# Score matmuls of both kinds in the two row halves, plain fp32 down products, and the gate copied by ScalarE and weighted by GpSimd

## The reference

```python
xn = layernorm(x)                                   # over the 128 channels
qkv = xn @ Wqkv + bqkv                              # 16 heads of depth 8
q, k = rope(q), rope(k)
scores = einsum('bhtd,bhsd->bhts', q, k) / sqrt(8)
attn = einsum('bhts,bhsd->bhtd', softmax(scores), v)  @ Wout + bout
r = sigmoid(xn @ gate_w + gate_b); top 2 of 16, values divided by their sum
hg, hu = xn @ experts_wg, xn @ experts_wu           # 16 experts of width 64
expert = sum over the two of r * ((silu(hg) * hu) @ experts_wd)
out = x + attn + xn + shared_mlp(xn) + expert       # shared_mlp: one more of width 64
```

## Time and profile before

| | |
|---|---|
| median of 3 runs | 239.06 us |
| the profiled execution | 239.08 us, of it 237.2 us span |
| TensorE busy | 212.7 us, 90% |
| VectorE busy | 186.9 us, 79% |
| GpSimd busy | 162.5 us, 69% |
| ScalarE busy | 135.3 us, 57% |
| chain that ended last | 64% TensorE, 18% VectorE |

### The profile page before, as it was taken

The page is one execution under the profiler, slowest core; times in us unless marked ns, Lnnn a source line. Parts: engine busy times, 40 slices in busy tenths (PEclk is TensorE's granted clock), DMA queues, the critical chain, the costliest instruction groups (busy, mean ns, idle before and its releaser), DMA issues.

```text
span 237.2 us, 4808 instructions
## 1 busy us (share of the span) xinstructions
PE 212.7 (90%) x1603; PEld 138.2 (58%) x1603; DVE 186.9 (79%) x407; ACT 135.3 (57%) x253; POOL 162.5 (69%) x245
## 2 busy tenths in 40 slices
PE   0485698889999999999999999999999999999993
PEld 0254454365565666665755656766766666676651
DVE  5897959999886888999858778998688878876521
ACT  2476111244458656665574766667676767666662
POOL 9185764799825479968938586979885874648722
PEclk9998789999999999999999999999999999999999
DMA  7924444630537340503662423206425550311101
GB/s 224 368 69 141 115 141 131 194 121 0 164 95 220 92 136 5 155 0 94 199 195 58 149 59 104 53 26 192 135 61 166 170 153 9 91 41 52 48 3 44
DMA packets 35953, 26.53 MB, mean 112 GB/s; under 512 B 4236, under 2 KB 30156, under 8 KB 35916
## 3 DMA queue, kind: packets, MB, share of 16 engines
q1 hardware_dynamic: 35292, 25.33, 35.9%
q10 hardware_dynamic: 636, 0.88, 1.0%
HBM read 18.53 MB, written 7.47 MB: 110 GB/s over the span
## 4 chain that ended last, share of the span: by engine, by line
PE 64%; DVE 18%; DMA 5%; SPq 4%; issue 3%; ACT 3%; POOL 1%; DVEq 0%; ACTq 0%; POOLq 0%
PE PV L553 11%; PE S2b L534 6%; PE S2a L534 5%; PE S1a L513 4%; DVE mx L1019 4%; PE S1b L513 4%; PE FB L391 3%; PE FA L393 3%; PE FA L391 3%; PE FA L392 3%; PE FB L393 3%; PE Y L391 3%; PE FB L392 3%; PE Y L392 2%; PE Y L393 2%
## 5 line engine op out<-in xcount | busy, mean ns | idle before, releaser
L749 ACT ACTIVATE probs<-S2b 128x512 f32<-128x512 f32 x62 | 37.0, 596 | 31.0 <-PE S2b L534 30.8
L1154 POOL TENSOR_TENSOR hid_lo<-gu,hid_hi 128x512 fp32r<-128x512 f32 (+1 forms) x27 | 34.7, 1286 | 23.5 <-ACT hid_hi L792 21.7
L1019 DVE TENSOR_REDUCE mx<-S1b 128x2 f32<-128x512 f32 x63 | 43.1, 684 | 7.8 <-PE S1b L513 7.7
L1019 DVE TENSOR_REDUCE mx<-S1a 128x2 f32<-128x512 f32 x65 | 44.5, 684 | 5.7 <-PE S1a L513 5.7
L1138 POOL TENSOR_TENSOR gu<-gu,wbc 128x512 f32<-128x512 f32 x32 | 41.0, 1282 | 11.5 <-DVE gu L1007 9.2
L749 ACT ACTIVATE probs<-S2a 128x512 f32<-128x512 f32 x62 | 37.1, 599 | 14.3 <-PE S2a L534 11.7
L553 PE MATMUL PV<-probs,vx 128*32 128x256 f32 x512 | 35.0, 384 | 0.9 <-ACT probs L749 0.9
L761 ACT ACTIVATE th<-FA 128x512 f32<-128x512 f32 (+1 forms) x36 | 21.5, 596 | 25.1 <-PE FA L393 24.8
L1028 DVE SCALAR_TENSOR_TENSOR th<-th,FA 128x512 f32<-128x512 f32 (+1 forms) x36 | 24.6, 683 | 10.9 <-ACT th L761 10.1
L513 PE MATMUL S1a<-k_hat,q_hat 96*128 96x256 bf16 x130 | 25.3, 275 | 0.7 <-DVE mx L1019 0.7
L513 PE MATMUL S1b<-k_hat,q_hat 96*128 96x256 bf16 x126 | 24.3, 273 | 1.4 <-DVE mx L1019 1.3
(11 more groups left out here) (171 smaller groups left out, 437.8 us busy)
## 6 DMA issues: line engine op xcount, KB each, us to landing
wbc<-route_w SPq DMA_DIRECT2D x64, 128.0 KB, 3.0
q_hat<-q_parts SPq DMA_DIRECT2D x32, 96.0 KB, 2.6
k_hat<-k_parts SPq DMA_DIRECT2D x32, 96.0 KB, 2.6
k_parts<-parts SPq DMA_DIRECT2D x8, 192.0 KB, 2.1
q_parts<-parts SPq DMA_DIRECT2D x8, 192.0 KB, 2.2
x_sb<-in_x SPq DMA_DIRECT2D x4, 256.0 KB, 4.1
q_parts<-parts SPq DMA_DIRECT2D x8, 128.0 KB, 2.1
k_parts<-parts SPq DMA_DIRECT2D x8, 128.0 KB, 2.1
```

What stands on the lines that cost most here:

```text
L749: nc.scalar.activation(probs[:, head % (2 * NQ), :], exp_bank(head)[:], ACT.Exp, scale=SCALE).then_inc(exp_done, 1)
L1019: nc.vector.tensor_reduce(mx[:, (q // QB) % 2, (q // 2) % 2, :, q % 2, i], S1[use % 2][:].rearrange("p (t s) -> p t s", t=SB), axis=AX.X, ...
L1154: nc.gpsimd.tensor_tensor(hid_lo[0:rows, m % 2, :], gu[0:rows, m % GU_SLOTS, :], hid_hi[0:rows, m % 2, :].bitcast(f32), ALU.subtract).then ...
```

## The change

- `k_hat` loses its copy for each parity and the zeros. A head's 48 score rows plus 3 rows of maxima or ones (`KALL` = 51) stand in rows 0 to 50 or in rows 64 to 114; which half is `score_row_half(q, i)`, so it alternates from step to step. The ones and the maxima take two DMAs each where they took one.
- TensorE issues a step's scores interleaved: first half of exp, first half of max, second half of exp, second half of max. The head of the maxima is the step's neighbour (`i ^ 1`), so that the two kinds read opposite row halves. Both banks are waited for ahead of the first of the four. Blocks 30 and 31 interleave two exponential heads.
- `down` is a plain fp32 matmul for all 36 chunks; `wd_hi`, `wd_lo`, `hid_hi`, `hid_lo` and what makes them are gone.
- From chunk 6 on, ScalarE copies FA to `gate` after the tanh (times 0.5 for c = 0) and with that frees FA; VectorE does one operation, (tanh + 1) * hu; GpSimd multiplies `gate` by the routing weight and then the product by `gate`.

```diff
-MROW = 2 * KROWS
+HROWS = 64
+KALL = KROWS + PARTS
...
+GATES_COPIED = CHLEAD
...
+def score_row_half(q, i):
+
+    return (q + i) % 2
...
-                sp.dma_start(k_hat[MROW:KALL, s], kones).then_inc(ld_kones, 16)
+                for r in range(2):
+                    sp.dma_start(k_hat[HROWS * r + KROWS:HROWS * r + KALL, s], kones).then_inc(ld_kones, 16)
...
-                sp.dma_start(q_hat[MROW:KALL, (h // 2) % 2, NQ * half:NQ * (half + 1), :],
-                             mT[0:MROWS * NQ, h % 2, :]).then_inc(max_ld[h % 4], 16)
+                for r in range(2):
+                    sp.dma_start(q_hat[HROWS * r + KROWS:HROWS * r + KALL, (h // 2) % 2, NQ * half:NQ * (half + 1), :],
+                                 mT[PARTS * NQ * r:PARTS * NQ * (r + 1), h % 2, :]).then_inc(max_ld[h % 4], 16)
...
+            def max_scores(bank, q, i, t):
+
+                j = i ^ 1
+                pair, slot, rows = NQ * ((q // 2) % 2) + j, (q // QB) % 2, HROWS * score_row_half(q, j)
+                return nc.tensor.matmul(bank[:, t * T:(t + 1) * T],
+                                        q_hat[rows:rows + KROWS, slot, pair, t * P:(t + 1) * P],
+                                        k_hat[rows:rows + KROWS, slot, pair, :], start=True, stop=True)
...
+            def exp_scores(bank, q, i, s):
+                pair, slot, rows = NQ * ((q // 2) % 2) + i, (q // QB) % 2, HROWS * score_row_half(q, i)
+                return nc.tensor.matmul(bank[:, s * T:(s + 1) * T],
+                                        k_hat[rows:rows + KALL, slot, pair, s * P:(s + 1) * P],
+                                        q_hat[rows:rows + KALL, slot, pair, :], start=True, stop=True)
+
+            def score_step(e, q, i):
+
+                exps, maxima = 0 <= e < FOUR_BANKS, 0 <= q < NBLK
+                if exps:
+                    s2 = free_exp_bank(e, i)
+                if maxima:
+                    s1 = max_bank(q, i)
+                for half in range(SB):
+                    if exps:
+                        scored = exp_scores(s2, e, i, half)
+                        if half == SB - 1:
+                            scored.then_inc(s2_ready, 1)
+                    if maxima:
+                        scored = max_scores(s1, q, i, half)
+                        if half == SB - 1:
+                            scored.then_inc(s1_ready, 1)
...
-                if n < PLAIN:
-                    pe.wait_ge(gu_weighted, n + 1)
-                    nc.tensor.matmul(Y[:], wd_sb[0:rows, c, :], gu[0:rows, n % GU_SLOTS, :],
-                                     start=c == 0, stop=c == NCH - 1).then_inc(down_done, 1)
-                    return
...
-                pe.wait_ge(hid_ready, n + 1 - PLAIN)
-                split_product(Y[:], wd_hi[0:rows, c, :], wd_lo[0:rows, c, :], hid_hi[0:rows, n % 2, :],
-                              hid_lo[0:rows, n % 2, :], c == 0, c == NCH - 1).then_inc(down_done, 1)
+                pe.wait_ge(gu_weighted, n + 1)
+                nc.tensor.matmul(Y[:], wd_sb[0:rows, c, :], gu[0:rows, n % GU_SLOTS, :],
+                                 start=c == 0, stop=c == NCH - 1).then_inc(down_done, 1)
...
-            act.wait_ge(ld_down, 32)
-            nc.scalar.activation(wd_hi[0:I, 0, :], wd_sb[0:I, 0, :], ACT.Copy)
-            nc.scalar.activation(wd_hi[:, 1:, :], wd_sb[:, 1:, :], ACT.Copy).then_inc(down_hi_ready, 1)
...
+                        if n >= GATES_COPIED:
+                            if n - 2 >= GATES_COPIED:
+                                act.wait_ge(gu_weighted, n - 1)
+                            nc.scalar.activation(gate[0:rows, n % 2, :], FA[0:rows, :], ACT.Copy,
+                                                 scale=0.5 if n % NCH == 0 else 1.0).then_inc(fa_read, 1)
...
-                        act.wait_ge(gu_weighted, n)
-                        if n - 3 >= PLAIN:
-                            act.wait_ge(down_done, n - 2)
-                        nc.scalar.activation(hid_hi[0:rows, (n - 1) % 2, :], gu[0:rows, (n - 1) % GU_SLOTS, :],
-                                             ACT.Copy).then_inc(hid_hi_ready, 1)
...
-            nc.vector.memset(k_hat[0:MROW, 0].rearrange("p a r t -> p (a r t)").bitcast(u32), 0).then_inc(hat_zeroed, 1)
...
+                            nc.vector.scalar_tensor_tensor(gu[0:rows, m % GU_SLOTS, :], th[0:rows, m % 2, :], 1.0,
+                                                           FB[0:rows, :], ALU.add, ALU.mult).then_inc(fb_read, 1)
...
-                    if i == 0 and n < NCHUNKS:
+                    if i == 0 and n < GATES_COPIED:
...
-            nc.gpsimd.memset(k_hat[0:MROW, 1].rearrange("p a r t -> p (a r t)").bitcast(u32), 0).then_inc(hat_zeroed, 1)
...
+            def weight_gate_and_product(m):
+
+                g, c = chunk_group(m)
                 rows = I if c == 0 else P
...
+                gates, product = gate[0:rows, m % 2, :], gu[0:rows, m % GU_SLOTS, :]
+                pool.wait_ge(fa_read, A_USE["hg", m] + 1)
+                if c:
+                    pool.wait_ge(wbc_ld[c - 1], 32 * (g + 1))
+                    after(nc.gpsimd.tensor_tensor(gates, gates, wbc[:, g % 2, c - 1, :], ALU.mult))
+                pool.wait_ge(fb_read, B_USE["hu", m] + 1)
+                nc.gpsimd.tensor_tensor(product, product, gates, ALU.mult).then_inc(gu_weighted, 1)
...
-                if PLAIN <= m < NCHUNKS:
-                    rows = I if m % NCH == 0 else P
-                    pool.wait_ge(hid_hi_ready, m + 1 - PLAIN)
-                    nc.gpsimd.tensor_tensor(hid_lo[0:rows, m % 2, :], gu[0:rows, m % GU_SLOTS, :],
-                                            hid_hi[0:rows, m % 2, :].bitcast(f32), ALU.subtract).then_inc(hid_ready, 1)
```

More of the change, by code:

```diff
@@ L186, in layer_kernel @@
         q_hat = sb("q_hat", [P, 2, H // 2, T], bf16)
-        k_hat = sb("k_hat", [P, 2, H // 2, 2, T], bf16)
+        k_hat = sb("k_hat", [P, 2, H // 2, T], bf16)
         mx = sb("mx", [P, 2, 2, SB, 2, NQ])
@@ L198, in layer_kernel @@
         th = sb("th", [P, 2, GT])
+        gate = sb("gate", [P, 2, GT])
         gu = sb("gu", [P, GU_SLOTS, GT])
-        hid_hi, hid_lo = sb("hid_hi", [P, 2, GT], f32r), sb("hid_lo", [P, 2, GT], f32r)
         yT = sb("yT", [P, 2, GT])
@@ L322, in load_hats @@
                 sp.wait_ge(scratch_done[slot], 16 * WRITES * (b // GB + 1))
-                if h < 4:
-                    sp.wait_ge(hat_zeroed, 2)
-                else:
+                if h >= 4:
                     sp.wait_ge(s2_ready, 2 * NQ * (h - 3))
                 for r in range(2):
-                    rows = slice(KROWS * r, KROWS * (r + 1))
+                    rows = slice(HROWS * r, HROWS * r + KROWS)
                     pairs = slice(NQ * half, NQ * (half + 1))
-                    for hat, dram in ((q_hat[rows, slot, pairs, :], q_dram), (k_hat[rows, slot, pairs, r, :], k_dram)):
+                    for hat, dram in ((q_hat[rows, slot, pairs, :], q_dram), (k_hat[rows, slot, pairs, :], k_dram)):
                         sp.dma_start(hat, dram[b, 2 * half + r].rearrange("j k t -> k j t")).then_inc(hat_ld[h % 4], 16)
@@ L504, in maxima_to_rows, with max_bank, free_exp_bank @@
                 last.then_inc(s1_ready, 1)
-            def max_scores(q, i):
-                b, r, hg = q // QB, q % 2, (q // 2) % 2
-                pair, slot = NQ * hg + i, b % 2
+            def max_bank(q, i):
                 if q % 2 == 0 and i == 0:
                     pe.wait_ge(hat_ld[(q // 2) % 4], 64 * (q // 8 + 1))
[L511 to L519, removed]
+                return take_s(("max", q * NQ + i))
+            def max_scores(bank, q, i, t):
[4 more added lines that the diff above has]
+                                        k_hat[rows:rows + KROWS, slot, pair, :], start=True, stop=True)
+            def free_exp_bank(q, i):
+                head = q * NQ + i
                 if q % 2 == 0 and i == 0:
-                    pe.wait_ge(max_ld[(q // 2) % 4], 16 * (q // 8 + 1))
+                    pe.wait_ge(max_ld[(q // 2) % 4], 32 * (q // 8 + 1))
                     if q == 0:
-                        pe.wait_ge(ld_kones, 32)
+                        pe.wait_ge(ld_kones, 64)
                         pe.wait_ge(spare_v_read, 1)
@@ L532, in exp_scores, with last_scores @@
                     pe.wait_ge(exp_done, head - 3)
[L533 to L537, removed]
+                return exp_bank(head)
+            def exp_scores(bank, q, i, s):
[18 more added lines that the diff above has]
+                            scored.then_inc(s1_ready, 1)
+            def last_scores(q):
+                for first in range(0, NQ, 2):
+                    banks = [free_exp_bank(q, first + k) for k in range(2)]
+                    for s in range(SB):
+                        for k in range(2):
+                            scored = exp_scores(banks[k], q, first + k, s)
+                            if s == SB - 1:
+                                scored.then_inc(s2_ready, 1)
```

(9 more changed lines are left out.)

80 lines of the change are left out of this document (30 added, 50 removed).

## The result

The changed kernel takes 244.26 us (median of four, 243.27 to 244.83) against 239.08 us: a ratio of 1.0208, interval 1.0171 to 1.0246. The profiled execution is 244.36 us (span 242.5), 5.3 us over the one of before; the sum said 5.9.

The account below looks back on a forecast made before the run. TensorE's queue was taken as the bound in the main stretch. The terms -24.6 + 21.6 + 4.5 - 0.9 + 1.5 + 1.7 + 4.1 - 2.0 = +5.9 us gave 245.0 us; forecast's own range 242 to 249, wider range 235 to 254.

Parts of the forecast that it names:

- The bound: In the main stretch, 57.17 to 219.69 us, TensorE bounds the kernel, with 2.25 us of idle time.
- Part 1: Exp and max scores in opposite row halves overlap fully, saving 0.22 us a step in blocks 0 to 27: -24.6 us.
- Part 2: Switches between 64-row scores and wide work cost time: +21.6 us in blocks 0 to 27, +4.5 us for EARLY_B items.
- the item behind them pays: Three shared-chunk down products now adjoin scores in the same mode; the next item pays the mode switch: -0.9 us.
- Part 3: Down as two plain fp32 instructions instead of three fp32r ones takes 0.15 us longer in 27 chunks: +4.1 us.
- Part 4: Gate work moved from VectorE to ScalarE and GpSimd removes TensorE waits: -2.0 us, bounds -2.25 and +3.
- Start: Blocks -4 to -1, maxima alone, pay mode switches: +1.7 us, bounds 0 and 3.3; zeroing of `k_hat` worth 0.
- pay the same passages with no gain: Blocks 28 and 29 have exponentials alone and pay 0.77 us each for mode switches without overlap gain: +1.5 us.
- A: Mode switches between scores and wide work are cheaper, so faster: 233 to 240 us, chance 0.19; free, below 233, 0.05.
- B: Row halves overlap only in part, 249 to 256 us, chance 0.15; not at all, 269.6 us, chance 0.05.
- C: New waits for gate copies or both score banks: +3 us, 248 to 250 us; counted within the forecast's 0.54.

Follow-up runs that it names:

- the kernel without the overlap: Changed kernel with all score matmuls reading the same row half, so exp and max scores cannot run side by side; 267.43 us in one execution.
- with hu: Changed kernel with the hu matmuls moved ahead of the scores of step 3 instead of behind them; 245.75 us.
- with an item: Changed kernel with the EARLY_B items of blocks 0 to 29 moved behind step 2, next to the down product; 242.9 us.
- The gate's change alone: Kernel before with the changes of the down products and the gate, scores as before; 243.76 us, ratio 1.0121.
- the two moves: Changed kernel with hu ahead of step 3 and the EARLY_B items behind step 2, from block 0 on; 241.94 us, ratio 1.0112.

## Why the prediction was right, step by step

**The sum.** Its terms are right in kind and nearly all in size, but that the total came within 0.6 us is in part luck. By stretch, the same terms give +1.4 us for the start, +2.4 for the main stretch and +2.1 for the tail; measured are +2.7, +1.5 and +1.1. The start was 1.3 us too low and the rest 1.9 us too high.

**The bound.** Right. TensorE led in the main stretch before and after; its idle time fell to 1.1 us, and the chain is 80% TensorE.

**Part 1, -24.6 us.** Right in full: 0.22 us a step in the timeline, and 23.7 us over the main stretch's 107 steps by the kernel without the overlap. That was chosen by the nearness of `attend`, and it held. The Trainium skill's 3.07x of four ("TensorE: Matmul & The Clock Gate", Measured speedup vs the span model) would have been 0.29 us a step as an estimate; its span model, nearly ideal, is what two row halves show, with 0.22.

**Part 2, the passages.** Right in size where they lead to wide work: 0.29 us per item between scores, given back each time one went (0.30 with hu, 0.29 with an item, 0.60 with both). Block 18 shows the sum of terms: 5.24 us before, 5.53 after, +0.29, where -0.88 + 0.77 + 0.25 + 0.15 = +0.29. The way in is 0.20 us from the last score to a wide matmul instead of 0.03, or of 0.11 where a plain fp32 matmul or a transpose follows. One detail was off. Of the shared chunks, those of blocks 14 and 23 have scores on both sides of the 64-row down, so no wide item pays behind it: blocks 14 and 23 went from 5.52 to 5.22 and from 5.33 to 4.80 us, and "the item behind them pays" cost the sum about 0.6 us too much. The price of a transpose item held in sum and not in its split: the first transpose starts 0.09 us later behind the scores, not 0.15 as read from a 64-row fp32 down, but the second follows it 0.05 us later than before and the scores behind come 0.10 later. Two transposes cost 0.24 us, a single one 0.21, against 0.25, and all 18 items together 4.4 us against 4.5.

**Part 3, down in plain fp32.** Right: +0.15 to 0.17 us in the places that compare, against 0.15.

**Part 4, -2.0 us for waits gone.** Right in size. By TensorE's idle time 1.1 us went. But a wait shows as idle only from the modelled end of the matmul ahead, so the starts say more: the wait below reads 0.75 us, and its place is 0.76 us shorter after although it holds a passage of 0.20 more, so 0.96 us of wait are gone.

```profile
130.72 0.42 PE L553 MATMUL PV<-probs,vx 128*32 128x256 f32 x4 [0.75 <-ACT probs L749]
```

Place by place, four waits of before are gone in the starts (0.96, 0.71, 0.23 and 0.14 us) and one of 0.12 has come, which makes 1.9 us. By the sum of the main stretch (-23.7 + 20.8 + 4.4 - 1.5 + 3.7 = +3.7 us against the measured +1.5) it is 2.2. The gate's change alone netted 1.3 (old waits gone, new ones for maxima come), and the scores' change alone added 1.6 us of idle time, so how the two share the gain isn't shown. In any case 22.5 us less on VectorE brought about a tenth of that.

**Start.** The passages of blocks -4 to -1 were taken at 1.7 us with bounds of 0 and 3.3; the start is 2.7 us longer, where all its terms gave 1.4. Not all of it is passages. The granted clock over the starts, after first and then before:

```profile
29.40:36.30 6.90, 6.90 (x24) 3.60 (x23) 3.21 (x6) 0.96 (x2) 4.17 (x6) 0.51 0.52 152
```

```profile
28.40:31.80 3.40, 3.32 (x9) 2.03 (x10) 2.50 (x4) 0.02 (x1) 2.27 (x5) 0.50 0.03 10
31.80:36.30 4.50, 4.50 (x29) 2.42 (x28) 2.57 (x4) 0.96 (x2) 2.71 (x4) 1.00 0.77 223
```

After spent 6.9 us at half clock with TensorE full, before 3.4. The sum had no term for that. What it costs can be estimated from after's own executions: the one of 243.27 us had a mean granted clock of 0.983, the other three 0.975 or 0.976 and 244.16 to 244.83 us. The difference in the mean is some 3.5 us at half clock, and 0.9 to 1.6 us of time. So the clock explains about the 1.3 us by which the start missed its terms. That is not closed: the means don't say where in the execution the clock was low, and the scores' change alone had 3.4 us at half clock, like before, and still came to the cut at 60.34, with 1.9 us of waits for maxima ahead of exps. The kernel without the overlap can't separate the two either: it kept the full clock from 25.0 us on and reached the cut at 58.29 us, 1.1 over before, but it lacks the 0.22 us in each of the five steps with both kinds that stand ahead of the cut.

**Tail.** It is +1.1 us. The terms gave +2.1: 1.5 for the passages of blocks 28 and 29, and 4 x 0.15 for downs. The term that failed is the one for blocks 28 and 29, which "pay the same passages with no gain". The steps 1 and 2 of these blocks are neighbours, and their exponentials read opposite halves, so they go side by side as well:

```profile
220.79 0.28 PE L538 MATMUL S2b<-q_hat,k_hat 51*128 51x256 bf16 x1
220.80 0.28 PE L538 MATMUL S2a<-q_hat,k_hat 51*128 51x256 bf16 x1
220.91 0.27 PE L538 MATMUL S2b<-q_hat,k_hat 51*128 51x256 bf16 x1
220.92 0.27 PE L538 MATMUL S2a<-q_hat,k_hat 51*128 51x256 bf16 x1
```

That is worth 0.22 us in each of the two blocks. Of blocks 30 and 31, put at 0 with a bound of -0.9, the first has its eight exponentials and the wait behind them in 0.54 us instead of 0.98, the second in 1.16 instead of 1.32. Together these are 1.0 us, the whole difference.

**The rivals.** A fell: its condition was a mean passage under 0.12 us, and the excursions of hu and down show 0.29 for two. B fell by the kernel without the overlap. C did not show in the full kernel, but it is what each further saving ran into: the two moves remove 0.60 us a block and of the possible 13 us (0.29 x 27 for hu and 0.29 x 18 for the items is 13.0) 10.9 leave TensorE's busy time, 5.4 come back as idle time, and 5.5 arrive.

## What to carry to other kernels

Where TensorE is the bound, count its changes of tile mode as instructions with a price: here about 0.29 us for a wide item between 64-row scores and 0.77 us a block, which ate nearly all of a real gain of 0.22 us a step, 0.88 a block. Group the work of one mode before splitting a step into smaller tiles. And when a queue is shortened, look at which engine's answer comes late next: the two moves brought waits of up to 2.4 us for VectorE's maxima, and in two runs a wait of nearly 2 us was followed by a stretch at half clock.

## What the runs showed of the hardware that I had not expected

- Matmuls in different row halves start out of their order in the queue: max 0.12 us ahead of an exp that precedes it (above). The Trainium skill, "TensorE: Matmul & The Clock Gate", The mechanism, says of matmuls that they are a "strict FIFO, no reordering"; for two disjoint row halves this trace shows otherwise in the starts (163.01 and 163.13 us). The ends are modelled in the records, and no run here tests them.
- Two halves side by side hardly slow each other: two matmuls that start together are followed by the next two after 0.12 us (161.51 and 161.63), and single ones follow each other at 0.11 us (the kernel without the overlap).
- A wait of 1.92 us in a stretch with little work was followed by 3.4 us at the 1.2 GHz level, in the middle of a stretch at full clock, and that block took 2.7 us more in all. The scores' change alone with both moves has a wait of 1.74 us, for maxima too, and 3.4 us at that level behind it. But a wait of 2.38 us in the first of these places, in the run with both moves, was not followed by a fall.
